# The delta-rule recurrence: P summed in PSUM from the decayed state and a Gram product, state brought up once in 32 steps

## The reference

```
S = S * a[t]                        # decay, per value channel
u = beta[t] * (v[t] - k[t] S)       # the update (delta)
S = S + k[t] (outer) u
o[t] = q[t] S
```

## Time and profile before

| | us |
|---|---|
| runs | 3885.35, 3885.53, 3891.2 (median 3885.53) |
| profiled execution | 3905.55 |
| its span | 3903.7 |
| stage of the recurrence, first to last L1205 | 2151.6 |
| TensorE, VectorE, ScalarE, GpSimd busy in the span | 3235.9, 2966.4, 2046.9, 2186.5 |

### The profile page before, as it was taken

The page is one execution under the profiler, slowest core; times in us unless marked ns, Lnnn a source line. Parts: engine busy times, 40 slices in busy tenths (PEclk is TensorE's granted clock), DMA queues, the critical chain, the costliest instruction groups (busy, mean ns, idle before and its releaser), DMA issues. The chain is left out here.

```text
span 3903.7 us, 126246 instructions
## 1 busy us (share of the span) xinstructions
PE 3235.9 (83%) x53441; PEld 2428.0 (62%) x53441; DVE 2966.4 (76%) x6600; ACT 2046.9 (52%) x4394; POOL 2186.5 (56%) x2735
## 2 busy tenths in 40 slices
PE   4688888888888888888888854869999899898989
PEld 2566666666667667666766643636666567656765
DVE  4488888888888888888888872058888788847884
ACT  2334444444444444444444423338787699728982
POOL 1367777767677676767777763420100188508860
PEclk7888998898898988989888975979999899999999
DMA  2111111111111111111111104100000012101111
GB/s 74 31 42 39 35 45 32 47 37 41 41 30 49 33 44 39 42 41 30 42 32 41 36 26 137 43 22 2 2 2 2 20 28 45 32 18 28 40 36 27
DMA packets 155957, 140.03 MB, mean 36 GB/s; under 512 B 64976, under 2 KB 108236, under 8 KB 155138
## 3 DMA queue, kind: packets, MB, share of 16 engines
q1 hardware_dynamic: 153090, 129.25, 12.1%
q0 software_dynamic: 2304, 2.71, 0.2%
HBM read 96.12 MB, written 16.82 MB: 29 GB/s over the span
## 5 line engine op out<-in xcount | busy, mean ns | idle before, releaser
L1238 DVE TENSOR_TENSOR a_tmp<-a_h,banks 128x128 f32<-128x128 f32 (+6 forms) x896 | 436.0, 487 | 29.8 <-DVE a_h L1215 0.2
L1244 DVE TENSOR_REDUCE a_h<-a_tmp 128x64 f32<-128x128 f32 (+6 forms) x896 | 432.2, 482 | 8.8
L694 PE MATMUL banks<-a_wt,a_kt 32*64 32x64 f32 x8192 | 190.3, 287 | 202.5 <-DVE a_wt L1281 202.5
L694 PEld LDWEIGHTS banks<-a_wt,a_kt 32*64 32x64 f32 x8192 | 178.5, 192 | 236.4 <-DVE a_wt L1281 236.4
L943 POOL TENSOR_TENSOR a_st<-a_st,a_ab 128x512 f32<-128x512 f32 x256 | 322.6, 1282 | 0.0
L2108 ACT ACTIVATE c_s<-c_s,c_low 128x384 f32<-128x384 f32 (+1 forms) x512 | 266.3, 579 | 19.0 <-DVE c_low L2052 13.6
L552 PEld LDWEIGHTS banks<-a_xseg,a_w_k 128*128 128x128 f32 x2048 | 236.2, 192 | 51.6 <-ACT a_va L776 29.9
L552 PE MATMUL banks<-a_xseg,a_w_k 128*128 128x128 f32 x2048 | 248.3, 278 | 20.7 <-DMA a_xseg<-xn 18.3
L2052 DVE CUSTOM_DVE_ANT_0 c_s<-banks,c_band 128x384 f32<-128x384 f32 (+1 forms) x512 | 245.5, 517 | 23.5 <-PE banks L1977 23.5
L2153 POOL TENSOR_TENSOR c_qm<-c_qT,c_heads 128x512 f32<-128x512 f32 x32 | 33.3, 1042 | 396.2 <-PE banks L1977 395.8
L958 POOL TENSOR_TENSOR a_h<-a_h,a_a 128x128 f32<-128x128 f32 (+3 forms) x256 | 142.2, 555 | 190.1 <-DVE a_h L1244 186.9
(11 more groups left out here) (318 smaller groups left out, 8791.6 us busy)
## 6 DMA issues: line engine op xcount, KB each, us to landing
a_ab<-decays SPq DMA_DIRECT2D x512, 128.0 KB, 3.0
d_Vs<-d_V SPq DMA_DIRECT2D x128, 128.0 KB, 2.3
sent<-k_nothing SPq DMA_DIRECT2D x40, 64.5 KB, 2.5
b_xe<-sent SPq DMA_DIRECT2D x8, 322.5 KB, 3.2
a_xseg<-xn SPq DMA_DIRECT2D x32, 70.0 KB, 2.5
a_xrow<-in_L_attn_x SPq DMA_DIRECT2D x128, 16.0 KB, 1.7
x<-a_xrow SPq DMA_DIRECT2D x128, 16.0 KB, 1.5
back<-k_nothing SPq DMA_DIRECT2D x32, 64.0 KB, 1.6
```

Of the source, the lines that this page charges most:

```text
L694: t = e.matmul(self.ubank(bi)[par * DK:(par + 1) * DK, ct * DK:(ct + 1) * DK], self.Kt[rows, k0:k0 + DK], self.Wt[rows, x:x + 2, :].rearra ...
L1238: e.tensor_tensor(prod, both, gram, ALU.mult).then_inc(*step.at((g, t, "product")))
L1244: e.tensor_reduce(self.results(ch, t), prod, AX.X, ALU.add).then_inc(*step.at((g, t, "w")))
```

## The change

- P of a chunk is now summed in PSUM from two products. pe_past_state multiplies the keys and queries with the decayed old state (which holds nothing of the chunk just done), and pe_past_chunk adds a Gram product of the last chunk's keys with this chunk's keys and queries, times the last chunk's turned updates. Only the second waits for the turned updates.
- The Gram matrices for that are Gn: Gn[0], between the two chunks of a segment, is copied out of the existing Gram product by act_gram; Gn[1], between a segment and the next one's first chunk, needs a product of its own (pe_next_gram, act_next_gram), which passes through banks 0 and 1.
- U, the carry, the evacuation and the addition run once in a segment. U stands behind the next segment's first P in TensorE's order, and its second pair of batches now uses banks 4 and 5. The addition (dve_add) runs at step 4 of the next even chunk. GpSimd multiplies the even chunk's updates by the odd chunk's decays ahead of the last transposition (pool_past) and clears them after it (pool_clear).
- The projection of q is cut in three (2, 3 and 3 of 8 tiles, of which the last two lie in the odd chunk; it was 4 and 4). The gates and the turned output move into the even chunk's dve_cross, the values' transposition to right behind the last one of the odd chunk. The projection and sigmoid of g move to the even chunk, one segment later; the scaling of the output moves to the even chunk; the order on all engines is adapted.

```diff
     def ubank(self, n):
-        return self.c.bank((6, 7, 2, 3)[n])
+        return self.c.bank((6, 7, 4, 5)[n])
...
+    def pe_next_gram(self, e, q, s, par):
+
+        b = self.take(q, ("next", s, par))
+        kq, nkq, ps = self.kq[s % 2], self.kq[(s + 1) % 2], slice(par * DK, (par + 1) * DK)
+        q.wait_ge(self.s_evac, ("k", s + 1, 1))
+        q.wait_ge(self.s_evac, ("q", s + 1, 2))
+        for ct in range(NCT):
+            for bi in range(NB):
+                r = ct * NB + bi
+                t = e.matmul(b[bi * SEG:(bi + 1) * SEG, ct * 2 * CK:(ct + 1) * 2 * CK], kq[ps, r, :, 0],
+                             nkq[ps, r, 0:CK].rearrange("p t z -> p (t z)"), start=True, stop=True)
...
-    def pe_P(self, e, q, s, ch):
...
+    def pe_past_state(self, e, q, g):
...
         for pair in range(0, NB, 2):
             if g:
-                q.wait_ge(self.s_st if pair else self.s_state, (g - 1, pair + 1))
+                q.wait_ge(self.s_decay, (g - 1, pair))
+                q.wait_ge(self.s_decay, (g - 1, pair + 1))
             for ct in range(NCT):
                 for bi in (pair, pair + 1):
                     for par in range(2):
                         ps, at = slice(par * DK, (par + 1) * DK), par * BANK + ct * DK
                         t = e.matmul(pb[bi * SEG:(bi + 1) * SEG, at:at + DK], kq[ps, ct * NB + bi, js].rearrange("p t z -> p (t z)"),
-                                     self.ST[ps, bi * NCT + ct, :], start=True, stop=True)
+                                     self.ST[ps, bi * NCT + ct, :], start=(ct == 0), stop=(g == 0 and ct == NCT - 1))
+        if g == 0:
+            t.then_inc(*self.s_p.at(0))
+
+    def pe_past_chunk(self, e, q, g):
+
+        s, ch = divmod(g, 2)
+        pb = self.c.bank(4, 2)
+        if ch:
+            q.wait_ge(self.s_evac, ("gram", s, 1))
+        else:
+            q.wait_ge(self.s_evac, ("next", s - 1, 1))
+        q.wait_ge(self.s_wt, g - 1)
+        for ct in range(NCT):
+            for par in range(2):
+                x, at = 16 * par + 2 * ct, par * BANK + ct * DK
+                for bi in range(NB):
+                    rows = slice(bi * SEG, (bi + 1) * SEG)
+                    t = e.matmul(pb[rows, at:at + DK], self.Gn[1 - ch][rows, 8 * par + ct, :],
+                                 self.Wt[rows, x:x + 2, :].rearrange("p h i -> p (h i)"), start=False, stop=(ct == NCT - 1))
         t.then_inc(*self.s_p.at(g))
...
-    def pe_carry(self, e, q, g):
...
+    def pe_carry(self, e, q, s):
...
-    def pe_U(self, e, q, s, ch):
...
+    def pe_U(self, e, q, s):
...
+        q.wait_ge(self.s_wt, 2 * s + 1)
         for pair in range(0, NB, 2):
             if pair:
-                q.wait_ge(self.s_step, (g, "last", "q"))
+                q.wait_ge(self.s_p2, 2 * s + 2)
             else:
-                q.wait_ge(self.s_carried, (g, 1))
+                q.wait_ge(self.s_carried, (s, 1))
...
-            self.pe_P(e, q, s, 0)
+            if old >= 0:
+                self.pe_U(e, q, old)
             for n in range(2):
                 self.pe_time_rows(e, q, s, n)
-            if old >= 0:
-                self.pe_moment(e, q, old, "mean")
-            for n in range(2):
-                if older >= 0:
-                    self.pe_turn(e, q, older, n)
             if more:
                 for half in range(2):
                     self.pe_project_rows(e, q, "a", nxt, half)
-                self.pe_project(e, q, "k", nxt, 0)
+            if older >= 0:
+                for n in range(2):
+                    self.pe_project(e, q, "g", older, n)
+            if old >= 0:
+                self.pe_moment(e, q, old, "mean")
             self.pe_cross(e, q, s, 0)
+            if older >= 0:
+                for n in range(2):
+                    self.pe_turn(e, q, older, n)
             if more:
-                self.pe_project(e, q, "k", nxt, 1)
+                for part in range(2):
+                    self.pe_project(e, q, "k", nxt, part)
                 self.pe_project(e, q, "q", nxt, 0)
-            self.pe_carry(e, q, g)
-            self.pe_U(e, q, s, 0)
-            g += 1
-            self.pe_P(e, q, s, 1)
+            self.pe_past_state(e, q, g + 1)
+            self.pe_past_chunk(e, q, g + 1)
             if more:
-                self.pe_project(e, q, "q", nxt, 1)
+                for part in range(1, 3):
+                    self.pe_project(e, q, "q", nxt, part)
                 for n in range(2):
                     self.pe_gram(e, q, nxt, n)
             if old >= 0:
                 self.pe_moment(e, q, old, "dev")
-            if older >= 0:
-                self.pe_out(e, q, older)
+            if more:
+                for n in range(2):
+                    self.pe_next_gram(e, q, s, n)
             self.pe_cross(e, q, s, 1)
             if more:
                 for half in range(2):
                     self.pe_project_rows(e, q, "v", nxt, half)
-            self.pe_carry(e, q, g)
-            if old >= 0:
-                for n in range(2):
-                    self.pe_gate(e, q, old, n)
-            self.pe_U(e, q, s, 1)
+            if older >= 0:
+                self.pe_out(e, q, older)
+            if more:
+                self.pe_past_state(e, q, g + 2)
+                self.pe_carry(e, q, s)
+                self.pe_past_chunk(e, q, g + 2)
...
+            q.wait_ge(self.s_p, 2 * s - 1)
+        e.activation(self.Gn[0][:, heads, :], self.held(("gram", s, par)).rearrange("p (r x) -> p r x", r=NCT)[:, :, SEG:], ACT.Copy,
+                     scale=1 / 8).then_inc(*self.s_gahead.at((s, par)))
...
+    def act_next_gram(self, e, q, s, par):
...
                 for n in range(2):
                     self.act_gram(e, q, nxt, n)
-            if older >= 0:
-                self.act_out(e, q, older)
+                for n in range(2):
+                    self.act_next_gram(e, q, s, n)
...
+
+    def past_part(self):
+        return self.H[:, :, SEG:SEG + CK]
+
+    def pool_past(self, e, q, s):
+
+        by = self.last[s % 2][:, 1, :].rearrange("p (i o) -> p i o", o=1).broadcast_to([P, 32, CK])
+        q.wait_ge(self.s_step, (2 * s, CK - 1, "w"))
+        q.wait_ge(self.s_hist, (2 * s, "whole"))
+        q.wait_ge(self.s_cum, (s, "last"))
+        q.wait_ge(self.s_wm, 2 * s + 1)
+        e.tensor_tensor(self.past_part(), self.H[:, :, 0:CK], by, ALU.mult).then_inc(*self.s_past.at(s))
+
+    def pool_clear(self, e, q, s):
+        q.wait_ge(self.s_wt, 2 * s + 1)
+        e.memset(self.past_part(), 0.0).then_inc(*self.s_clear.at(s))
...
             self.pool_rest(e, q, s, 0)
             self.pool_history(e, q, s, 0, HAND, HC)
+            if older >= 0:
+                self.pool_scale(e, q, older)
             self.pool_second_half(e, q, s, 0)
-            for n in range(2):
-                self.pool_decay(e, q, g, n)
+            if old >= 0:
+                self.pool_clear(e, q, old)
             self.pool_cross(e, q, s, 0)
             self.pool_first_half(e, q, s, 0)
-            for n in range(2):
-                if old >= 0:
-                    self.pool_centre(e, q, old, n)
-            for n in range(2, 4):
+            for n in range(4):
                 self.pool_decay(e, q, g, n)
             self.pool_query(e, q, s, 0)
             self.pool_prepare(e, q, s, 1)
-            for half in range(2):
-                if older >= 0:
+            if old >= 0:
+                for n in range(2):
+                    self.pool_centre(e, q, old, n)
+            if older >= 0:
+                for half in range(2):
                     self.pool_gate(e, q, older, half)
             g += 1
             self.pool_rest(e, q, s, 1)
@@ -1121,21 +1200,21 @@
                 if more and t > HAND:
                     self.pool_cumulate(e, q, nxt, t - HAND - 1, t - HAND)
             self.pool_second_half(e, q, s, 1)
-            for n in range(2):
-                self.pool_decay(e, q, g, n)
+            if more:
+                for n in range(2):
+                    self.pool_decay(e, q, g, n)
+                self.pool_cumulate(e, q, nxt, 3, 5)
             self.pool_cross(e, q, s, 1)
             self.pool_first_half(e, q, s, 1)
-            for n in range(2, 4):
-                self.pool_decay(e, q, g, n)
             if more:
-                self.pool_cumulate(e, q, nxt, 3, HC)
+                self.pool_past(e, q, s)
+                for n in range(2, 4):
+                    self.pool_decay(e, q, g, n)
             self.pool_query(e, q, s, 1)
-            if old >= 0:
-                self.pool_scale(e, q, old)
             if more:
+                self.pool_cumulate(e, q, nxt, 5, HC)
+                self.pool_gram_rows(e, q, nxt)
                 self.pool_prepare(e, q, nxt, 0)
-                self.pool_gram_rows(e, q, nxt)
-            if more:
                 self.pool_values(e, q, nxt)
             if older >= 0:
                 self.pool_add(e, q, older)
...
             if t == HAND:
```

(44 more changed lines are left out.)

138 lines of the change are left out of this document (77 added, 61 removed).

## The result

The changed kernel took 3960.79 us (median of 4 runs, 3939.41 to 3969.15) against 3887.7 for the kernel before: +73 us by the medians; the ratio of the runs is 1.0165, 95% interval 1.0144 to 1.0187 (here and in the table below it is not the plain quotient of the medians). The profiled execution took 3969.15 us, with a span of 3967.4. The forecast was 3842.5 us, its range ended at 3925. So a segment takes 70.6 us instead of 68.3, where 66.9 was forecast.

The account below looks back on a forecast made before the run. No engine was full; dependences between engines, with VectorE carrying the recurrence, set the pace. Even 31.6 plus odd 35.3 gave 66.9 against 68.3 us a segment, -43 us in all: 3842.5 us, own range 3825 to 3870, range 3780 to 3925.

Parts of the forecast that it names:

- The boundary: Between chunks: after the transposed updates, a 64-matmul product of 2.06 us replaces U, evacuation and P; clock 1.0 there.
- upper bound of the product: At the boundary: the new product at half clock, by U's ratio, takes 3.6 us.
- The DMAs are the same: Whole stage: DMAs unchanged, as the decays' broadcast follows the cumulation by over 20 us.
- Late next: Odd chunk, GpSimd: work behind X starts 3.8 us later and would be late next, by 0 to 1 us.
- The odd chunk's layout: Odd chunk: X (cross product taken back) at 17.6 us, VectorE ends it at 33.9; with the clock's 1.4, 35.3.
- half of a full slowing: Odd chunk: a clock fall slows half Gram and cross product, 2.75 us if all slowed, on average half, 1.4.
- The sum: Per segment: 31.6 even plus 35.3 odd, 66.9 against 68.3 us; -1.4 in 31 segments, -43 us.
- The first: Rival, odd chunk: the clock never falls there, 65.5 us a segment, -87 us, 3798.5; chance 0.20.
- second: Rival, even chunk: TensorE's waits for evacuations are shorter, VectorE's 30.6 ends it; -118 us, 3767.5; chance 0.10.
- The third: Rival, odd chunk: every fall slows all of half Gram and cross product, X at 20.3; -3 us, 3882.5; chance 0.13.
- The fourth: Rival, even chunk: waits around the turn drop the clock at k, 3.4 us lost; +62 us, 3947.5; chance 0.15.
- what would make it wrong: Wrong as a whole if GpSimd or a DMA ends the wait at VectorE's P transposition or the first addition.

Follow-up runs that it names:

- e1: Changed kernel with the load of a segment's input issued two segments ahead, before the decays' broadcast instead of behind broadcast and stores: 3918.69 us.
- e9: Changed kernel with the state's part of the odd chunk's P (128 small matmuls) before the q projection's first part (16 long ones): 3917.22 us.
- e4: Changed kernel with the odd chunk's cross product ahead of the next Gram product on TensorE, and VectorE turning the Gram rows behind X: 3884.62 us.
- e2: Changed kernel with VectorE turning the values behind the output's subtraction in the odd chunk instead of ahead of it: 3961.29 us.
- e8: Changed kernel with GpSimd's scaling of the values cut to one column of 32 in every segment but the first (a probe, output differs): 3958.26 us.
- e14: Changed kernel with e1, e4, e9 and e2 together, plus the next Gram product's first half before the odd chunk's cross product: 3815.3 us.
- e15: Changed kernel with e1, e4, e9, the next Gram's first half before the odd cross product, and values taken early on VectorE and GpSimd: 3822.31 us.
- e6: Changed kernel with the first half of the next Gram product computed four times instead of once in odd chunks: 4084.02 us.
- e16: Changed kernel with 9 throwaway identity matmuls filling TensorE's wait before the odd chunk's cross product: 3956.77 us.

## Why the prediction was wrong, point by point

- **The boundary: right.** The new product took 1.97 to 2.12 us where it had no gap and 2.06 was taken, the state part 1.9 (2.0), U 1.16 a half (1.0), and the clock was 1.00 over 1344.0 to 1352.3. Gn[0]'s copy took 0.39, the clearing 0.53 (0.5), GpSimd's product of past updates 1.06 (1.28). (A slip without effect: by U's ratio the upper bound of the product is 3.45 us, not 3.6.)
- **"The DMAs are the same": the step that failed in the even chunk.** I wrote that the decays' broadcast follows the cumulation by over 20 us. That holds for the broadcast in the middle of the even chunk only. The other one started 1.6 us after the cumulation's end (1235.66 to 1237.26 in the rows above), and the load of x stands behind it in SyncE's queue, and the cumulation was among the work that I myself had moved 3.8 us later. Late next, "by 0 to 1 us", was the sentence that should have been carried through the queue. By those rows it had 4.3 us to spare; the cumulation ended 10.7 us before the next P then and 5.7 now. Price 1.8 us at X, with the clock's fall that the wait brings; e1 took it away.
- **A term that was not in the sum, the other step that failed there: the supply of instructions.** I took the durations of small matmuls from rows where they stood alone and put 128 + 128 of them in a row. Price 1.2 us before the even chunk's P; e9 took it away. The kernel before had the sign: gaps named "issue" before matmuls, added up over the waits from 150 to 2370 us, of 33.0 us (41 times), and 96.9 (105 times) after. That sum is not the price: in e4 it grew to 166.7 us, and the kernel became 76 us shorter.
- **The odd chunk's layout: right in X, 1.0 short at the end.** X at 18.9 for 19.0, TensorE's idle time before the second half 2.62 for 2.75. That X fits to 0.1 us is in part luck: the second half started at 14.2 instead of 14.75, and the low clock cost 1.9 us (0.3 in the half Gram product, 1.6 in the cross product) instead of the 1.4 that half of a full slowing gave. The end missed the subtraction's 1.3 us beside GpSimd's values. Its size was wrong by that, but without effect on the total by e2, e8, e14 and e15: take it away, and the even chunk waits instead.
- **The sum.** 1.8 + 1.2 + 1.0, less 0.1 at the odd X, is 3.9 us a segment over the forecast; 31 times 3.9 is 121, and -43 + 121 = +78, with 72 measured in the stage.
- **The rivals.** The first and second are out. The third had the right behaviour of the clock (the whole cross product slowed, in 29 of 31 segments) at too high a price, X at 20.3 for 18.9; by its time, 3882.5, it is out. The fourth gave 3947.5 and the time came near it, by another mechanism: k ran in 7.41 us for 64 records at a clock of 1.00, so its fall at k did not happen. The clock did fall in the even chunk, at the a rows, behind a wait for a DMA that the layout did not have. The forecast said what would make it wrong: a DMA that ends a wait. I had named the wrong wait.
- **What the change itself costs.** By e4 the order of two products on TensorE and of one transposition on VectorE is worth 76 us, and the change lost 73: with both mended it stands level with the kernel before.

## What to carry to other kernels

When work is shifted later, follow every in-order queue that waits for it to its end, SyncE's too, and ask what unrelated load stands behind. Count instructions and not only busy time on TensorE: two runs of 128 small matmuls are better with something long between them (e9). A stall that a trace shows (a contention, a slow clock) is worth what the next wait behind it allows; here removing the contention five times and the slow clock once brought nothing, and the order of work brought 148 us.

## What the runs showed of the hardware that I had not expected

- TensorE's instructions come in packets of 16.4 KB, never less than 3.2 us apart here, and runs of small matmuls (12 to 16 ns a record) use them up faster: gaps of 1.1 to 1.9 us, 128 records apart (e6), each ending 1.2 to 1.6 us after a packet.
- Because of it the clock is not always worth its price: the odd chunk's cross product took 3.64 us at the low clock (median, the change) and 3.76 at the full one with its gap (e16).
- A VectorE instruction with two SBUF inputs took 2.43 us instead of 1.1 beside a GpSimd product of 2.36 us.
